# State-space layer and ternary feed-forward on eight cores: first product of block pairs as seven half-size products, one ring of x buffers, second rounding on ScalarE

## The chip, the cores and the metric

The kernel runs as one program on the 8 cores (NeuronCores) of one Trainium2 chip. The metric is the device time of one execution in microseconds (us), taken on the slowest core. A core has TensorE (matmuls into PSUM), VectorE (DVE in the profile), ScalarE (ACT), GpSimd (POOL) and SyncE (SP), each with its own in-order instruction stream; they meet through semaphores. A wait in a stream holds up all that is queued behind it.

## What is computed

x is 4 sequences of 8192 tokens by D = 1024, f32. The reference, cut to what matters:

```python
x = x + attn(layernorm(x))       # u = x W_in^T (N = 64); h_t = Abar h + Bbar u_t; y = (C h) W_out^T
x = x + ffn(layernorm(x))

def quant_weight(w):             # ternary: -s, 0, +s
    s = clip(mean(abs(w)), EPS, None)
    return clip(round(w / s), -1, 1) * s
def quant_act(x):                # integers -127..127 with a scale for each token
    scale = 127 / clip(max(abs(x), axis=-1), EPS, None)
    return round(x * scale) / scale
def ffn(x):                      # 1024 -> 4096 -> 1024
    h = gelu(quant_act(x) @ quant_weight(w1).T)
    return quant_act(h) @ quant_weight(w2).T
```

## The kernel before

Each sequence is split over two cores. The even core owns its first 33 blocks of 128 tokens (FIRST), the odd core the other 31 (LATER). The odd core first computes the state that the scan starts from with 33 short steps over the first part's x. After that all cores do the same: load and make ternary both weight matrices (as FP8, in units of 2^-9), and then pass over their blocks.

One block c takes these steps, and each engine's program is an order written out by hand:

- `stats(c)` (VectorE, 528): mean and variance; `inv1` (GpSimd): the power -0.5; `xnorm(c)` (ScalarE, 393): normalized x in BF16; `txn(c)` (SP, 205): its DMA transposition.
- `mmu(c)` (TensorE, 763): u; `scan(c)` (VectorE, 546); `hbf(c)` (ScalarE, 400): the state in BF16; `mmy(c)` (TensorE, 773, 774): y.
- `mix(c)` (VectorE, 550 to 579): x2 = x + y into a buffer of its own, its statistics, row maximum, scale, and rounding by adding and subtracting 1536 in F16, to `k1`; `inv2_` on GpSimd stands within it; `tk1(c)` (SP, 211): DMA transposition.
- `mm1(c)` (TensorE, 751): eight groups of 512 output columns, eight matmuls each (128x128 stationary, 512 columns), over three PSUM banks; `gelu(c, gi)` (ScalarE, 380) takes each group out into `h`.
- `hmax(c, j)` (VectorE, 583): row maximum of 1024 columns of h; `hquant(c)` (VectorE, 588 to 601): a chain of five small operations for the scale, then `k2h` (599: multiply, add 1536, 4096 columns) and `k2b` (601: subtract); `tk2(c)` (SP, 219): DMA transposition.
- `mm2(c)` (TensorE, 786): 32 x 2 matmuls of 512 columns into `pout` (two banks); `fin(c)` (VectorE, 607): x2 + a2 * pout, stored by GpSimd (318).

From block 2 on TensorE runs `mm1(b)`, `mmu(b+2)`, `mmy(b+1)`, `mm2(b-1)`. Blocks 0 and 1 and the weights are interleaved ahead of that. VectorE runs `fin(b-2)`, `stats(b+3)`, four `hmax(b)`, `mix(b+1)`, `scan(b+2)`, `hquant(b)`. x is loaded by GpSimd (297) into a ring of three buffers and x2 goes into a ring of four. `mm2(c)` waits until `fin(c-1)` has read `pout`.

All buffers in SBUF are views into one array, `BIG`, so that is the name that most rows show; PSUM tensors are `pm` (first product), `pout`, `py`, `pu`.

Of the kernel before, what the change touches and what calls it, by code (L numbers as in the profile page):

```python
# [26 lines left out]
VE_TILES = (0, 4)  # L27


def build_nc():  # L30
# [42 lines left out]
    xbs = [at(28, D), at(96, D), at(100, D)]  # L73
    x2 = [at(176, D), at(180, D), at(48, D), at(104, D)]
# [6 lines left out]
    k1he, k1hs = at(168, D, F16), at(56, D, F16)  # L81
    k1be = [at(170, D, BF16), at(188, D, BF16)]
    k1bs = [at(58, D, BF16), at(60, D, BF16)]
    k1T = [at(184 + 2 * i, D, BF16).rearrange("p (k t) -> p k t", k=8) for i in range(2)]
    k2h = [at(188, H, F16), at(64, H, F16)]
    k2b = [at(188, H, BF16), at(64, H, BF16)]
    k2T = [at(o, H, BF16).rearrange("p (m t) -> p m t", m=32) for o in (32, 72)]

    def xb_of(c):
        return xbe[c] if c < 2 else xbs[(c - 2) % 3]  # L90
# [34 lines left out]
    amx, cl, rr, q1, am2, cl2, r2, sc2 = [s1(34 + i) for i in range(8)]  # L125
    am4 = s1(42, 4)
# [13 lines left out]
    pm1 = [nc.alloc_psum_tensor(f"pm1{i}", [128, 512], F32).ap() for i in range(3)]  # L140
    pout = nc.alloc_psum_tensor("pout", [128, 1024], F32).ap()
# [10 lines left out]
            + ["xe0", "xe1"] + [f"xl{i}" for i in range(3)] + [f"od{i}" for i in range(4)]  # L152
            + [f"{n}{i}" for n in ("xT", "kT", "hT") for i in range(2)]
            + ["id", "pxn", "exn", "pk1", "ek1"])

    with ExitStack() as ctx:
# [15 lines left out]
        def wait_xb(eng, c):  # L172
            if c < 2:
                eng.wait_ge(S[f"xe{c}"], 16)
            else:
                eng.wait_ge(S[f"xl{(c - 2) % 3}"], 16 * ((c - 2) // 3 + 1))


        def sync_program(sp, later):
# [40 lines left out]

            tk2(0)
# [6 lines left out]
            for b in range(2, own):  # L228
                if b + 3 < own:
                    txn(b + 3)  # L230
                if 4 <= b + 1 < own:
                    tk1(b + 1)
                tk2(b)

# [9 lines left out]
        def gpsimd_program(g, later):  # L244
# [6 lines left out]
            g.memset(tu, TU)  # L251
            g.iota(ident_f, pattern=[[-1, 128]], base=0, channel_multiplier=1,
# [58 lines left out]
            load(5)  # L311
            inv1(3)
            inv1(4)
            inv2_(3)
            for b in range(2, own + 2):
                c = b - 2
                g.wait_ge(S["out"], c + 1)
                g.dma_start(out=out_d[c], in_=x2[c % 4]).then_inc(S[f"od{c % 4}"], 16)  # L318
                if b + 3 < own:
                    inv1(b + 3)  # L320
                if 4 <= b + 1 < own:
                    inv2_(b + 1)
# [14 lines left out]
        def scalar_program(s, later):  # L337
# [120 lines left out]
            for b in range(2, own):  # L458
                for gi in range(4):
                    gelu(b, gi)  # L460
                if b + 3 < own:
                    xnorm(b + 3)
                for gi in range(4, 8):
                    gelu(b, gi)
                if b + 2 < own:
                    hbf(b + 2)
# [10 lines left out]
        def vector_program(v, later):  # L477
# [72 lines left out]
            def mix(c):  # L550
                v.wait_ge(S["y"], c + 1)
                xx = x2[c % 4]
                xc, k1h = (xce, k1he) if c < 2 else (xcs, k1hs)
                if c >= 4:
                    v.wait_ge(S[f"od{c % 4}"], 16 * (c // 4))
# [19 lines left out]
                v.tensor_scalar(k1h, xc, q1, MAGIC, op0=ALU.mult, op1=ALU.add); D_()  # L575
                if c >= 4:
                    v.wait_ge(S[f"kT{c % 2}"], 16 * (c // 2 - 1))
                v.tensor_scalar(k1b_of(c), k1h, -MAGIC, None, op0=ALU.add)
                D_().then_inc(S["k1"], 1)

            def hmax(c, j):
                v.wait_ge(S["gelu"], 8 * c + 2 * j + 2)
                v.tensor_reduce(am4[:, j:j + 1], h_of(c)[:, j * 1024:(j + 1) * 1024], AX.X,  # L583
                                ALU.max, apply_absolute_value=True)

            def hquant(c):
                D_()
                v.tensor_reduce(am2, am4, AX.X, ALU.max); D_()
# [297 lines left out]
```

## Time and profile before

| | |
|---|---|
| median of 3 runs | 1107.63 us (1107.47 to 1111.19) |
| profiled execution | 1110.62 us; span of its slowest core (6) 1109.1 us |
| even cores (33 blocks), spans | 1104.3, 1105.5, 1105.7, 1109.1 us |
| odd cores (31 blocks), spans | 1097.5, 1098.3, 1096.1, 1096.8 us |
| busy, core 6 | TensorE 88%, VectorE 63%, ScalarE 29%, GpSimd 10% |

The span runs from the first instruction of a core to its last. Busy shares are of the whole span. "Granted clock" is the share of full clock that TensorE was given in a stretch; 1.00 is 2.4 GHz and 0.50 is 1.2 GHz. In a row, L751 is line 751, `out<-in` names what is written and read, and the bracket says how long the engine was idle before and what ended that. A timeline merges instructions of one kind that follow each other; "x64" is their number. "SPq" is the queue of SyncE, whose time is the issue of a DMA, not its transfer.

### The profile page before, as it was taken

Reading aid. Unit: us, or ns where it says so; the run is one execution under the profiler, and the core shown is the slowest. Engines: PE = TensorE matmul, PEld = TensorE weight load, DVE = VectorE, ACT = ScalarE, POOL = GpSimd, SP = SyncE. Lnnn points to the kernel's source line nnn. Section 1 sums busy time; section 2 is a strip of 40 time slices with the busy share of each in tenths; the row PEclk is TensorE's granted clock in tenths of the full one; section 3 lists DMA queues with packets and bytes.
Section 4 is the critical chain, followed back from the end, with each engine's and each line's share of the span. In section 5 each row is a group of like instructions: output and inputs, shape, how many; then the busy total and the mean of one; then the engine's idle time right before and its main releaser. Section 6 shows DMA issues by size and latency. Waiting matters only on the chain.

```text
span 1109.1 us, 13658 instructions; the slowest of 8 cores (1096.1 to 1109.1 us)
## 1 busy us (share of the span) xinstructions
PE 970.7 (88%) x4590; PEld 436.2 (39%) x4590; DVE 695.9 (63%) x1050; ACT 323.3 (29%) x378; POOL 114.6 (10%) x187
## 2 busy tenths in 40 slices
PE   0116719899999999999999999999999999999995
PEld 0102204344444444444444444444444444444442
DVE  0257887686666666666666666666666666666630
ACT  2279972322222222222222222222222222222110
POOL 1004021111111111110011111111111100000000
PEclk9998859999999999999999999999999999999998
DMA  5946824344444434334444444444443333333340
GB/s 177 337 153 228 378 57 114 77 100 91 95 95 95 92 90 94 83 90 95 96 95 95 95 95 96 95 94 88 96 86 86 85 90 84 90 71 67 67 95 38
DMA packets 213950, 120.53 MB, mean 109 GB/s; under 512 B 203184, under 2 KB 203184, under 8 KB 211824
## 3 DMA queue, kind: packets, MB, share of 16 engines
q1 hardware_dynamic: 202352, 52.45, 25.8%
q0 software_dynamic: 11520, 67.11, 17.6%
q8 instruction: 40, 0.66, 0.2%
q14 instruction: 38, 0.31, 0.1%
HBM read 51.38 MB, written 17.30 MB: 62 GB/s over the span
## 4 chain that ended last, share of the span: by engine, by line
PE 82%; DVE 5%; ACT 4%; DMA 4%; issue 2%; ACTq 1%; DVEq 1%; SPq 1%; POOL 0%; POOLq 0%
PE pm L751 39%; PE pout L786 39%; DMA BIG<-woutT 3%; ACT BIG L361 2%; PE pu L763 2%; ACT BIG L366 1%; PE py L773 1%; DVE BIG L633 1%; ACTq L367 1%; PE py L774 1%; ACTq L363 1%; DMA BIG<-xh 1%; ACT BIG L380 0%; DVE BIG L628 0%; DVE BIG L629 0%
## 5 line engine op out<-in xcount | busy, mean ns | idle before, releaser
L751 PE MATMUL pm<-BIG 128*128 128x512 fp8e4 x2112 | 470.4, 384 | 19.6 <-DVE BIG L629 9.3
L786 PE MATMUL pout<-BIG 128*128 128x512 fp8e4 x2112 | 464.1, 380 | 22.8 <-DMA BIG<-BIG 20.0
L751 PEld LDWEIGHTS pm<-BIG 128*128 128x128 bf16 x2112 | 207.8, 99 | 276.6 <-issue 34.4
L786 PEld LDWEIGHTS pout<-BIG 128*128 128x128 bf16 x2112 | 204.4, 98 | 279.6 <-issue 39.6
L583 DVE TENSOR_REDUCE sm<-BIG 128x1 f32<-128x1024 f32 x132 | 160.5, 1219 | 230.2 <-ACT BIG L380 230.2
L380 ACT ACTIVATE BIG<-pm,sm 128x512 f32<-128x512 f32 x264 | 179.9, 686 | 377.5 <-PE pm L751 376.1
L400 ACT CAST hb_s<-h_s 64x128 bf16<-64x128 f32 x33 | 9.8, 298 | 287.3 <-DVEq L548 287.3
L599 DVE TENSOR_SCALAR BIG<-BIG,sm 128x4096 f16<-128x4096 f32 x33 | 77.6, 2353 | 5.4 <-issue 1.0
L288 POOL TENSOR_TENSOR sm<-sm 128x1 f32<-128x1 f32 x33 | 28.3, 859 | 443.1 <-DVE sm L563 443.1
L607 DVE SCALAR_TENSOR_TENSOR BIG<-pout,sm,BIG 128x1024 f32<-128x1024 f32 x33 | 42.3, 1283 | 28.9 <-PE pout L786 22.9
L794 PE MATMUL pout<-BIG 128*128 128x128 bf16 x32 | 4.0, 305 | 61.5 <-ACT BIG L393 47.7
L318 POOL DMA_DIRECT2D out<-BIG x33 | 18.1, 549 | 361.7 <-DVE BIG L607 361.7
L393 ACT ACTIVATE BIG<-BIG,sm 128x1024 bf16<-128x1024 f32 x33 | 40.6, 1231 | 49.0 <-POOL sm L281 49.0
L361 ACT ACTIVATE BIG<-BIG 128x4096 fp8e4<-128x4096 f32 (+1 forms) x14 | 47.2, 3372 | 7.1 <-DMA BIG<-w1t 5.4
L366 ACT ACTIVATE BIG<-BIG,sm 128x4096 f32<-128x4096 f32 x12 | 45.6, 3798 | 6.4 <-DVEq L622 5.8
L601 DVE TENSOR_SCALAR BIG<-BIG 128x4096 bf16<-128x4096 f16 x33 | 40.5, 1227 | 4.3 <-issue 0.5
L565 DVE TENSOR_REDUCE sm<-BIG 128x1 f32<-128x1024 f32 x33 | 40.3, 1220 | 2.4
L556 DVE TENSOR_TENSOR BIG<-BIG,py 128x1024 f32<-128x1024 f32 x33 | 39.9, 1211 | 0.7 <-PE py L774 0.5
L633 DVE TENSOR_SCALAR BIG<-BIG 128x4096 fp8e4<-128x4096 f32 x12 | 27.5, 2294 | 6.7 <-ACTq L367 5.6
L279 POOL TENSOR_TENSOR sm<-sm 128x1 f32<-128x1 f32 x33 | 22.5, 682 | 81.4 <-DVE sm L538 81.4
L794 PEld LDWEIGHTS pout<-BIG 128*128 128x128 bf16 x32 | 3.1, 137 | 62.8 <-issue 62.8
L575 DVE TENSOR_SCALAR BIG<-BIG,sm 128x1024 f16<-128x1024 f32 x33 | 24.9, 753 | 2.5
(83 smaller groups left out, 389.4 us busy)
## 6 DMA issues: line engine op xcount, KB each, us to landing
out<-BIG POOLq DMA_DIRECT2D x33, 512.0 KB, 6.5
BIG<-w1t POOLq DMA_DIRECT2D x8, 2048.0 KB, 35.3
BIG<-w2t POOLq DMA_DIRECT2D x8, 2048.0 KB, 17.9
BIG<-xh POOLq DMA_DIRECT2D x31, 512.0 KB, 4.0
BIG<-BIG SPq DMA_TRANSPOSE x95, 3.1
BIG<-xh SPq DMA_DIRECT2D x2, 512.0 KB, 16.1
BIG<-winT SPq DMA_DIRECT2D x1, 256.0 KB, 25.6
BIG<-woutT SPq DMA_DIRECT2D x1, 256.0 KB, 30.4
```

The costliest lines, as they stand in the source:

```text
L361: s.activation(junk[:, 0:part], wtile[w][:, 0:part], AF.Abs, bias=0.0, scale=1.0, accum_out=acc[:, w:w + 1], saturate=False)
L366: s.activation(wtile[w], wtile[w], AF.Relu, bias=tu, scale=cw)
L380: s.activation(h_of(c)[:, gi * 512:(gi + 1) * 512], pm1[G % 3], AF.Gelu, bias=0.0, scale=a1[c % 4]).then_inc(S["gelu"], 1)
L393: s.activation(xn_of(c), xb_of(c), AF.Identity, bias=nb1[c % 2], scale=inv[c % 2]).then_inc(S["xn"], 1)
L556: v.tensor_tensor(xx, xb_of(c), py, ALU.add)
L565: v.tensor_reduce(amx, xc, AX.X, ALU.max, apply_absolute_value=True); D_()
L583: v.tensor_reduce(am4[:, j:j + 1], h_of(c)[:, j * 1024:(j + 1) * 1024], AX.X, ALU.max, apply_absolute_value=True)
L599: v.tensor_scalar(k2h[c % 2], h_of(c), sc2, MAGIC, op0=ALU.mult, op1=ALU.add)
L601: v.tensor_scalar(k2b[c % 2], k2h[c % 2], -MAGIC, None, op0=ALU.add)
L607: v.scalar_tensor_tensor(x2[c % 4], pout, a2[c % 4], x2[c % 4], op0=ALU.mult, op1=ALU.add).then_inc(S["out"], 1)
L751: m = t.matmul(pm1[G % 3], k1T[c % 2][:, k, :], t1T[gi][:, k, :], start=(k == 0), stop=(k == 7))
L786: i = t.matmul(pout[:, d * 512:(d + 1) * 512], k2T[c % 2][:, m, :], t2T[m // 4][:, m % 4, d * 512:(d + 1) * 512], start=(m == 0), stop=(m ...
```

## The change

It has three parts, all from block 5 (`PAIR0`) on, with new orders for blocks 2 to 4.

**Seven products.** Blocks are taken in pairs (c0, c1), 14 on an even core, 13 on an odd one. In the first product the pair's 256 tokens, the 1024 inputs and each 1024 output columns (group j of four) are cut in halves: a 2x2 by 2x2 block product, which is done with seven half-size products M1 to M7 in place of eight (Winograd's form of Strassen's method). Each is four matmuls of 512 columns (`prod`). The sums of x (`xsums`: four additions of 512 columns in F16 a pair, on VectorE) go into `sa`; the sums of weights (`wsums`, `wsum3`: four subtractions of 2048 FP8 columns for each j, once, on VectorE in blocks 2 to 4) into `tb`. Partial results are kept in h: ScalarE copies the bank `pp` out after M1, M6 and M7 (`sn1`, `sn2`, `sn3`), TensorE goes on accumulating in it, VectorE adds another bank to the copies (`add11`, `add22`, `add12`), and Gelu then works in place in SBUF (`g11`, `g22`, `g12`) or from the bank (`g21`).

**One ring of x.** `xs` has seven buffers, from the load through x2 and the result to the store; from block 7 on SP issues the loads. `mm2` uses two pairs of banks in turn.

**Second rounding on ScalarE.** The multiply-and-add of 4096 columns (599) becomes `k2round`, an ACTIVATE with bias 1536. k1 is transposed in F16, without a BF16 copy.

Cut to its core, with the orders that matter:

```diff
+PAIR0 = 5
+NX = 7
-    xbs = [at(28, D), at(96, D), at(100, D)]
-    x2 = [at(176, D), at(180, D), at(48, D), at(104, D)]
+    xs = [at(o, D) for o in (176, 180, 28, 48, 60, 96, 100)]
...
+    pout, pout2 = pw[:, 0:1024], pw[:, 1024:2048]
+    pm1 = [pw[:, 1024:1536], pw[:, 1536:2048], pr]
+    pp = [pw[:, 0:512], pw[:, 1024:1536]]
+    pq = [pw[:, 512:1024], pw[:, 1536:2048]]
...
# SyncE, in place of txn(b + 3), tk1(b + 1), tk2(b)
+            for q in range(pairs(own)):
+                txn(c1 + 2); load(c0 + 4); txn(c0 + 4); tk1(c0 + 2)
+                tk2(c0); tk1(c1 + 2); load(c1 + 4); tk2(c1)
...
# ScalarE
+            def k2round(c):
+                s.wait_ge(S["hs"], c - 1)
+                s.wait_ge(S[f"hT{c % 2}"], 16 * (c // 2))
+                s.activation(k2h[c % 2], h_of(c), AF.Identity, bias=magic,
+                             scale=sc2[c % 2]).then_inc(S["k2h"], 1)
+            def keep(g, src, dst, made, sem):
+                s.wait_ge(S[made], g + 1)
+                s.copy(dst, src).then_inc(S[sem], 1)
+                sn1(0) g11(0) sn2(0) sn1(1) sn3(0) g22(0) g11(1)
+                xnorm(c1 + 2)
+                sn2(1) g12(0) g21(0)
+                hbf(c0 + 2)
+                for j in (2, 3):
+                    sn3(j-1) sn1(j) g22(j-1) g11(j) sn2(j) g12(j-1) g21(j-1)
+                sn3(3) g22(3) g12(3) g21(3)
+                hbf(c1 + 2) xnorm(c0 + 4) k2round(c0) k2round(c1)
...
# VectorE
+            def wsums(j):
+                v.tensor_tensor(tb_f[j][0], b12, b11, ALU.subtract, saturate=False); D_()
+                v.tensor_tensor(tb_f[j][1], b22, tb_f[j][0], ALU.subtract, saturate=False); D_()
+                v.tensor_tensor(tb_f[j][2], b21, tb_f[j][1], ALU.subtract,
+                                saturate=False).then_inc(S["tsum"], 1)
+            def addto(g, c, j, d, src, made, kept, sem):
+                o = h_of(c)[:, j * 1024 + d * 512:j * 1024 + (d + 1) * 512]
+                v.wait_ge(S[made], g + 1)
+                v.wait_ge(S[kept], g + 1)
+                v.tensor_tensor(o, src, o, ALU.add).then_inc(S[sem], 1)
+            for b in range(2, PAIR0):
+                fin(b - 2)                          # from b = 3
+                stats(b + 3) hmax(b, 0) hmax(b, 1) scan(b + 2)
+                hmax(b, 2) hmax(b, 3) hscale(b) mix(b + 2) k2int(b)
+                b == 2: wsums(0) wsums(1)      b == 3: wsums(2) wsums(3)
+                b == 4: wsum3(0) wsum3(1) among the hmax, then wsum3(2) wsum3(3) xsums(0)
+            for q in range(pairs(own)):
+                fin(3 if q == 0 else c1 - 4)
+                add11(0) stats(c1 + 2) add22(0) scan(c0 + 2) add11(1) add12(0) add22(1)
+                add11(2) hmax(c0, 0) hmax(c1, 0) add12(1) add22(2)
+                add11(3) hmax(c0, 1) stats(c0 + 4) add12(2) hmax(c1, 1) add22(3)
+                scan(c1 + 2) hmax(c0, 2) add12(3) hmax(c1, 2) hmax(c0, 3)
+                hscale(c0) hmax(c1, 3) hscale(c1) mix(c0 + 2) k2int(c0)
+                fin(c0 - 2)                         # from q = 1
+                mix(c1 + 2) k2int(c1) xsums(q + 1)
...
# TensorE
+            for b in range(2, PAIR0):
+                mm1(b, 0, 4); mmu(b + 2); mm1(b, 4, 8); mmy(b + 2)
+                if b >= 3:
+                    mm2(b - 1)
+            def prod(bank, a, w, start, sem):
+                for k in range(4):
+                    m = t.matmul(bank, a[:, k, :], w[:, k, :], start=start and k == 0,
+                                 stop=k == 3, skip_group_check=not start)
+                m.then_inc(S[sem], 1)
+                m1(0) m5(0) m2(0) m6(0) m1(1) m7(0) mmu(c0 + 2) m5(1) m2(1) m6(1) m3(0) m4(0) m7(1)
+                for j in (2, 3):
+                    m1(j) m5(j) m2(j) m6(j) m3(j-1) m4(j-1) m7(j)
+                    if j == 2: mmy(c0 + 2)
+                mmu(c1 + 2) m3(3) m4(3)
+                mm2(c0 - 2, 0, 16) mmy(c1 + 2) mm2(c0 - 2, 16, 32) mm2(c1 - 2)
+                # q == 0: mm2(4) alone, with mmy(c1 + 2) in its middle
+            mm2(own - 2)
+            mm2(own - 1)
```

In the last pair the steps of blocks that do not exist are left out. What the seven products wait for: M1(0) of pair 0 for `fin(3)`, M1(1) for `fin(c1-4)`, M1(j) from j = 2 for g21(j-2); M5(0) for the first x sum, M5(j) from j = 2 for add12(j-2); M2(j) for add11(j-1); M6(j) for sn1(j); M7(j) for sn2(j); M3(j) for add22(j); M4(j) for sn3(j). `mm2(own-1)` no longer waits for `fin(own-2)`.

## Rows read from the trace of the kernel before

**Rows 1.** Busy time in a stretch (columns named in the first row), core 6.
```profile
core 6: us, PE busy (x) PEld busy (x) DVE busy (x) ACT busy (x) POOL busy (x), PEclk, DMA share, GB/s
308.00:1057.00 749.00, 749.00 (x3581) 338.15 (x3580) 490.44 (x769) 175.31 (x257) 69.17 (x123) 1.00 0.41 89
```
**Rows 2.** Timeline of one block on TensorE: start us, us, engine, line.
```profile
506.63 13.98 PE L751 MATMUL pm<-BIG 128*128 128x512 fp8e4 x64
...
520.53 0.63 PE L763 MATMUL pu<-BIG,winTb 128*64 128x128 bf16 x8
...
521.63 13.99 PE L786 MATMUL pout<-BIG 128*128 128x512 fp8e4 x64
...
535.46 13.98 PE L751 MATMUL pm<-BIG 128*128 128x512 fp8e4 x64
```
**Rows 3.** Groups by line: busy us, mean ns, idle before and releaser.
```profile
L380 ACT ACTIVATE BIG<-pm,sm 128x512 f32<-128x512 f32 x264 | 179.9, 686 | 377.5 <-PE pm L751 376.1 <-issue 1.4
L366 ACT ACTIVATE BIG<-BIG,sm 128x4096 f32<-128x4096 f32 x12 | 45.6, 3798 | 6.4 <-DVEq L622 5.8
L393 ACT ACTIVATE BIG<-BIG,sm 128x1024 bf16<-128x1024 f32 x33 | 40.6, 1231 | 49.0 <-POOL sm L281 49.0
L601 DVE TENSOR_SCALAR BIG<-BIG 128x4096 bf16<-128x4096 f16 x33 | 40.5, 1227 | 4.3 <-issue 0.5
L556 DVE TENSOR_TENSOR BIG<-BIG,py 128x1024 f32<-128x1024 f32 x33 | 39.9, 1211 | 0.7 <-PE py L774 0.5 <-issue 0.2
L546 DVE TENSOR_TENSOR_SCAN h_s<-abt,h_s,pu 64x128 f32<-64x128 f32 x32 | 15.1, 472 | 15.7 <-PE pu L763 8.5 <-issue 7.1
L404 ACT CAST BIG<-pout 128x1024 bf16<-128x1024 f32 x2 | 2.0, 1012 | 4.8 <-PE pout L794 4.8
```
**Rows 4.** Timeline of VectorE: stats and two hmax, then a mix and a scale.
```profile
209.07 0.69 DVE L531 BATCH_NORM_STATS2 sm<-BIG 128x6 f32<-128x512 f32 x1 [0.19 <-issue]
...
210.88 2.35 DVE L583 TENSOR_REDUCE sm<-BIG 128x1 f32<-128x1024 f32 x2
...
1041.60 1.21 DVE L556 TENSOR_TENSOR BIG<-BIG,py 128x1024 f32<-128x1024 f32 x1
...
1049.33 0.16 DVE L588 TENSOR_REDUCE sm<-sm 128x1 f32<-128x4 f32 x1 [0.17 <-issue]
...
1050.44 2.35 DVE L599 TENSOR_SCALAR BIG<-BIG,sm 128x4096 f16<-128x4096 f32 x1
```
**Rows 5.** Timeline where one engine hands over to another.
```profile
508.67 0.69 ACT L380 ACTIVATE BIG<-pm,sm 128x512 f32<-128x512 f32 x1 [6.13 <-PE pm L751]
...
510.34 0.69 ACT L380 ACTIVATE BIG<-pm,sm 128x512 f32<-128x512 f32 x1 [0.98 <-PE pm L751]
...
511.13 1.22 DVE L583 TENSOR_REDUCE sm<-BIG 128x1 f32<-128x1024 f32 x1 [0.81 <-ACT BIG L380]
...
1081.76 1.28 DVE L607 SCALAR_TENSOR_TENSOR BIG<-pout,sm,BIG 128x1024 f32<-128x1024 f32 x1 [6.91 <-PE pout L786]
...
1083.19 13.97 PE L786 MATMUL pout<-BIG 128*128 128x512 fp8e4 x64 [1.54 <-DVE BIG L607]
```
**Rows 6.** Timeline of blocks 2 and 5, and transposes by issue to landing (page).
```profile
200.33 12.26 PE L751 MATMUL pm<-BIG 128*128 128x512 fp8e4 x56
...
210.41 1.26 SPq L205 DMA_TRANSPOSE BIG<-BIG  x1
...
275.97 13.98 PE L751 MATMUL pm<-BIG 128*128 128x512 fp8e4 x64
...
BIG<-BIG SPq DMA_TRANSPOSE x95, 3.1
```
**Rows 7.** TensorE after waits, and stretches: cores 6 and 1.
```profile
163.22 12.73 PE L786 MATMUL pout<-BIG 128*128 128x512 fp8e4 x48 [19.97 <-DMA BIG<-BIG]
...
243.15 13.40 PE L751 MATMUL pm<-BIG 128*128 128x512 fp8e4 x56
...
240.00:245.00 5.00, 3.40 (x15) 1.35 (x16) 3.46 (x7) 0.30 (x2) 0.81 (x2) 0.71 0.02 3
...
195.00:200.00 5.00, 1.88 (x15) 0.89 (x13) 1.20 (x3) 0.30 (x1) 0.00 (x0) 1.00 0.27 52
```

More of the change, by code:

```diff
@@ L708, in vector_program @@
-                if 4 <= b + 1 < own:
-                    mix(b + 1)
-                if b + 2 < own:
-                    scan(b + 2)
-                if b < own:
-                    hquant(b)
+                stats(b + 3)
+                hmax(b, 0)
+                hmax(b, 1)
+                scan(b + 2)
+                if b == 4:
+                    wsum3(0)
+                hmax(b, 2)
+                if b == 4:
+                    wsum3(1)
+                hmax(b, 3)
+                hscale(b)
@@ new lines, in vector_program, with add11, add22, add12 @@
+                mix(b + 2)
+                k2int(b)
+                if b == 2:
+                    wsums(0)
+                    wsums(1)
+                elif b == 3:
+                    wsums(2)
+                    wsums(3)
+                else:
+                    wsum3(2)
+                    wsum3(3)
+                    xsums(0)
+            for q in range(pairs(own)):
+                c0, c1 = PAIR0 + 2 * q, PAIR0 + 2 * q + 1
+                def add11(j):
+                    addto(4 * q + j, c0, j, 0, pr, "M2", "sn1", "a11")
+                def add22(j):
+                    addto(4 * q + j, c1, j, 1, pq[j % 2], "M5", "sn3", "a22")
+                def add12(j):
+                    addto(4 * q + j, c0, j, 1, pq[j % 2], "M3", "sn2", "a12")
+                fin(3 if q == 0 else c1 - 4)
+                add11(0)
+                if c1 + 2 < own:
+                    stats(c1 + 2)
+                add22(0)
+                if c0 + 2 < own:
+                    scan(c0 + 2)
+                add11(1)
+                add12(0)
+                add22(1)
+                add11(2)
+                hmax(c0, 0)
+                hmax(c1, 0)
+                add12(1)
+                add22(2)
+                add11(3)
+                hmax(c0, 1)
+                if c0 + 4 < own:
+                    stats(c0 + 4)
+                add12(2)
+                hmax(c1, 1)
+                add22(3)
+                if c1 + 2 < own:
+                    scan(c1 + 2)
+                hmax(c0, 2)
+                add12(3)
+                hmax(c1, 2)
+                hmax(c0, 3)
+                hscale(c0)
+                hmax(c1, 3)
+                hscale(c1)
+                if c0 + 2 < own:
+                    mix(c0 + 2)
+                k2int(c0)
+                if q > 0:
+                    fin(c0 - 2)
+                if c1 + 2 < own:
+                    mix(c1 + 2)
+                k2int(c1)
+                if c1 + 2 < own:
+                    xsums(q + 1)
@@ L715, in _ @@
+            for c in range(own - 3, own):
+                fin(c)
         @block.vector
```

368 lines of the change are left out of this document (286 added, 82 removed).

## The prediction

> **What bounds the kernel now.** I read the stretches first: between 308 and 1057 us TensorE is busy in every microsecond at granted clock 1.00, VectorE 65% and ScalarE 23% [rows 1]. The timeline of one block then shows what TensorE does: first product from 506.63, u and y from 520.53, second product from 521.63, next block at 535.46, so 28.83 us a block; 64 matmuls of 512 columns go from 521.63 to 535.46, 0.216 us each [rows 2]. TensorE's work is the time there; the other engines and the DMAs are under it. So a matmul left out is worth 0.216 us, if nothing makes TensorE wait instead. The profiled core has 33 blocks, its odd-numbered neighbours 31 and a longer start; they end earlier and lose one pair less, so they don't set the time.
>
> **Sizes used for the new work.** One product of the seven is four matmuls: 0.86 us. A copy PSUM to SBUF of 512 columns ("keep"): the 1024-column one took 1.01 [rows 3]; bounds 0.51 (half) and 0.69 (the Gelu of as many columns); I take 0.59, since 1024 to 4096 columns cost 0.84 ns a column on ScalarE (lines 393, 366) and the rest is fixed. Gelu out of SBUF: 0.69 as out of PSUM [rows 3]; below 0.62 (half of line 393), above 0.80 (0.43 plus line 393's fixed 0.37). An addition of 512 columns: 0.68, from half of line 556's 1.21 (0.61) and VectorE's other 512-column operation, 0.69 [rows 3, 4]; I take the nearer to the latter. The rounding on ScalarE, 128x4096: 3.80, as line 366. On VectorE an operation that waits for nothing starts about 0.08 early: two hmax in 2.35, one 1.22, and stats holds the engine 209.07 to 210.88, 1.81. mix holds it 7.7 (1041.60 to 1049.33), the scale of a block 1.1 (to 1050.44) [rows 4], scan 0.65 (0.47 [rows 3] and its drain). Handovers: the eighth matmul's slot ends at 506.63 + 8 x 0.216 = 508.36 and Gelu starts 508.67, so 0.31; ScalarE to VectorE 0.10 (510.34 + 0.69 to 511.13), and I take the same back; VectorE to TensorE 0.15 (1081.76 + 1.28 to 1083.19) [rows 5].
>
> **The pair, saving.** Four column groups of seven products of four matmuls, 112, replace 128: 16 x 0.216 = 3.45 us a pair, 14 pairs, 48.3 us.
>
> **The pair, what it adds.** Before, TensorE fed three banks and only Gelu stood behind it. Now all engines work through written orders in which 12 keeps, 12 additions and 16 Gelus alternate, and TensorE waits for them. Each of the four column groups j holds one chain that starts at the end of M2(j), so their waits add up:
> - j=0: handover 0.31, add11 0.68, 0.10, g11 0.69, sn2 (queued behind g11) 0.51, 0.15 = 2.44, before M7(0). TensorE has M6 and M1(1), 1.73, in between: waits 0.7.
> - j=1: the same, with xnorm (1.15) ahead of sn2: 3.59, against M6, M3, M4 = 2.59: waits 1.0. Then g12(0) and g21(0) (1.22) before M1(2), against M7: 0.36.
> - j=2: 0.31, add11 0.68, two hmax and add12(1) 2.88, 0.10, g12 0.69, g21 0.61, 0.15 = 5.42, before M1(3). TensorE: four products and y, 3.92: waits 1.5.
> - j=3: 0.31, add11 0.68, then hmax, stats and add12(2) on VectorE 3.55, 0.10, g12 0.69, g21 0.61, sn3(3) 0.51, 0.10, add22(3) 0.68, 0.15 = 7.38, before M3(3). TensorE: four products and u, 4.02: waits 3.4. This is the largest: a 1.81 us stats that nobody waits for stands ahead of an addition that everybody waits for.
> - After the products y of the second next block needs x2 of the first, whose mix stands behind the rest of that queue: after add22(3) a scan, four hmax, add12(3), two scales and the x2 addition, 9.4. TensorE has M3, M4 and half an mm2, 8.8: waits 0.65.
>
> Together 7.55 against 3.45 saved: +4.1 us a pair. Hidden: both roundings on ScalarE, under the two second products (27.7 us); the four sums of transposed x (0.42 to 0.68 each), ready about 1 us before M5(0) wants them if the transposition lands in 3.1 us [rows 6] (if that cover goes, each us late is 13 us in all); the loads, which move from POOL's queue to SP's, where each stands behind transposes but has most of a pair before its stats; the second block's k1 transpose, which stands behind the k2 transpose of the first on SP, due 9 us before it. POOL keeps stores and powers, none of which TensorE waits for sooner than before. The x ring and second output bank remove waits that are nearly nil; the last one (1.5, ahead of 1083.19 [rows 5]) goes.
>
> **The change-over, blocks 2 to 4.** TensorE now wants u(4) after half of block 2's product. The transposition that it needs is issued at 210.41 [rows 6] and queued behind the same work as before, so it lands at 213.6 where TensorE stands at 200.33 + 6.9: about 6 us. The block's last Gelu then ends at 222.1, its scale at 224.6. From there VectorE is the bound. Up to fin(3), for which M1 of the first pair waits, its queue holds 3 mix 23.0, 3 conversions (line 601) 3.9, 16 subtractions of FP8 weights, 3 fin 3.7, 2 stats 3.6, 8 hmax 9.4, 2 scales 2.2, 2 scans 1.3, the x sums 1.8. A subtraction has 2048 columns and two sources: line 556 takes 1.21 for 1024, so 2.28 (2.3 with its drain); no row shows two-source FP8, and the bound below is half, since one-source operations do better than line 556 per column (line 601). Nearest is the two-source row: 36.8. In all 85.7, and 2.3 of waits (xnorm and Gelu behind stats): 312.8 for M1, where the first product of block 5 starts at 275.97 now [rows 6]: +36.9.
> The Trainium skill, VectorE: DVE Perf Modes, "What auto-detection actually checks", lets a two-source operation double its rate only if every tensor is 16-bit. By it the sum stands as made here; by the lower bound of the rows it would be 18.4 us smaller. No run yet shows which.
>
> **First and last pair.** Pair 0 has one second product instead of two under VectorE's two mixes: counted from the last product, mix starts at +6.1, and 7.7 + 1.3 + 7.7 + 3.1 + 0.7 (mix, conversion, mix, transposition, x sum with handover) end at +26.6; TensorE would be at M5(0) at 13.8 + 0.5 + 0.65 + 0.86, +15.8: waits 10.7. Pair 13 has no u, y, stats or xnorm: by the same chains 5.5 of waits.
>
> **Sum.** 36.9 + (4.1 + 10.7) + 12 x 4.1 + (5.5 - 3.45) - 1.5 = +101.4. The clock: after 20 us without work 48 matmuls took 12.73 instead of 10.35 [rows 7], 2.4 lost; two new long waits (about 8 and 11 us) have no other wait behind them: +4.8. Total +106.2. The profiled execution took 1110.62 (span 1109.1), so 1217; its distance to the median of 1107.63 is 3, so **1214**.
>
> **Rivals.**
> - *TensorE loses its clock in every pair.* Around M3(3) it has one u (0.57 us) in 3.9. For: on core 1 a like stretch ended at 243.15 with the clock at 0.71, and 56 matmuls took 13.40 for 12.26: with y 1.5 lost. Against: core 6 had the same waits at 195 to 200 and stayed at 1.00 (2.4 GHz; 0.50 is 1.2) [rows 7]. Price 1.5 to 2.4 x 12: 1232 to 1243. The Trainium skill, TensorE: Matmul & The Clock Gate, "HAM oscillation — how this bites in real kernels", has a loop pay in every iteration for waits that are long enough; no row here shows that in a steady loop. Chance 0.18.
> - *Cheap subtractions* (two columns a cycle, 1.14): 16 x 1.15 = 18.4 less, 1196. Only the missing row speaks for it. 0.11.
> - *Waits in the pairs half as long* (handovers shorter, operations overlapping more): 14 x 3.8 less, 1161. 0.10.
> - *TensorE stays the bound in the pairs*, the one that ends faster: each chain j is over before TensorE needs it, and 48.3 comes back in full. For: up to add12(3) VectorE has fin 1.2, 12 additions 7.7, 2 stats 3.6, 2 scans 1.3 and 5 hmax 5.9, 19.7 us, in 25.8 of products, so the load fits. Against: order, not load, makes the waits. With the change-over as above -2, 1105; with it at the lower bound 1087. It decides where the waits fall under 1.5 a pair. 0.09 (0.02 of it within 0.5%).
> - *Forecast* 0.52.
>
> **Numbers.** Unknown sizes move a pair by -1.1 (3 keeps, 5 Gelus, 7 additions in the chains at their lower bounds) to +0.9: 1199 to 1227; with the subtractions and the restarts at their least 1176; with the clock rival 1255. Down to 1160 the half-wait case is in. Range 1160 to 1255; outside remain the faster case and some 0.1 of worse. A measurement tells 0.5% (5.5 us) from no change. Faster 0.07, same 0.02, slower 0.91.
>
> **What would show it.** The step from one pair's first product to the next near 61.7 us; TensorE idle about 7.5 us in it, 3.4 of that ahead of the second-to-last product, released by add22; FP8 subtractions near 2.3 us; first pair's M1 near 313, M5(0) of the second pair 10 us late, released by VectorE. Wrong it is if a pair takes 57.7 or less, or if the subtractions take 1.2; a clock under 1.00 in the middle means the first rival.

## The result, and the profile after

The changed kernel takes 1220.98 us (median of 4 runs, 1218.05 to 1226.02), the kernel before on the same chip 1107.55 us (4 runs, 1106.08 to 1111.19): the ratio is 1.1024, 95% interval 1.0978 to 1.1069. It is slower by 113 us; forecast were 1214, between 1160 and 1255. The profiled execution, the slowest of the four, took 1226.02 us, span 1224.5 on core 4 (33 blocks); the even cores 1217.3 to 1224.5, the odd ones 1201.5 to 1203.6. Executions in which the cores of one die ran at a lower clock than the others stand in no ratio below; experiment 2's profile is of such a one, and is read on a core of the other die.

Busy shares of the whole span, from the page. TensorE was at 88% on the core profiled before; VectorE and ScalarE were at 63% and 29%.

```profile
PE 957.0 (78%) x4366; PEld 414.2 (34%) x4366; DVE 785.1 (64%) x1259; ACT 520.6 (43%) x577; POOL 101.6 (8%) x162
```

The same stretch view as [rows 1], over the pairs:

```profile
core 4: us, PE busy (x) PEld busy (x) DVE busy (x) ACT busy (x) POOL busy (x), PEclk, DMA share, GB/s
395.00:1040.00 645.00, 577.27 (x2663) 250.30 (x2662) 435.81 (x756) 278.05 (x354) 46.15 (x82) 0.97 0.38 83
```

TensorE, which was busy in every microsecond [rows 1], now stands idle for 68 of 645 us, and no other engine is busy all the time (VectorE 68%, ScalarE 43%). The granted clock is 0.97 and no longer 1.00.

One pair on TensorE, the view of [rows 2]: start us, us, engine and line (L1090 the seven products, L1010 and L1020 u and y, L1040 the second product), and in brackets the wait ahead and what ended it.

```profile
511.84 1.02 PE L1090 MATMUL pw<-BIG 128*128 128x512 fp8e4 x4 [0.75 <-ACT BIG L530]
...
518.69 1.02 PE L1090 MATMUL pw<-BIG 128*128 128x512 fp8e4 x4 [0.84 <-ACT BIG L530]
519.88 1.89 PE L1090 MATMUL pw<-BIG 128*128 128x512 fp8e4 x8 [0.17 <-ACT BIG L560]
...
527.89 1.89 PE L1090 MATMUL pw<-BIG 128*128 128x512 fp8e4 x8 [1.26 <-ACT BIG L560]
...
534.02 0.63 PE L1010 MATMUL pu<-BIG,winTb 128*64 128x128 bf16 x8
537.92 1.89 PE L1090 MATMUL pw<-BIG 128*128 128x512 fp8e4 x8 [3.26 <-DVE BIG L877]
...
547.21 0.37 PE L1020 MATMUL py<-woct,hb_s 64*128 64x512 bf16 x1 [0.50 <-DVEq L686]
```

These are the six waits of the forecast, in its order: 0.7, 1.0, 0.36, 1.5, 3.4 and 0.65 were forecast; 0.57 to 0.75, 0.84, 0.17, 1.26, 3.26 and 0.50 are there. L877 ahead of M3(3) is the addition add22(3). A pair whose clock holds takes 61.69 us (547.74 to 609.43, from the last 96 matmuls of its second products to those of the next pair), against 57.66 for two blocks before.

The change-over and the first two pairs, same view:

```profile
215.25 1.03 PE L1010 MATMUL pu<-BIG,winTb 128*64 128x128 bf16 x8 [7.70 <-DMA BIG<-BIG]
...
257.05 3.57 PE L998 MATMUL pw<-BIG 128*128 128x512 fp8e4 x8 [17.01 <-ACT BIG L430]
...
317.58 3.57 PE L1090 MATMUL pw<-BIG 128*128 128x512 fp8e4 x8 [6.45 <-DVE BIG L751]
...
350.41 1.89 PE L1090 MATMUL pw<-BIG 128*128 128x512 fp8e4 x8 [3.11 <-DVE BIG L877]
354.36 8.75 PE L1040 MATMUL pw<-BIG 128*128 128x512 fp8e4 x32 [2.06 <-ACT BIG L560]
...
379.19 1.86 PE L1090 MATMUL pw<-BIG 128*128 128x512 fp8e4 x4 [7.66 <-DVEq L867]
```

Block 5's first product, at 275.97 before [rows 6], starts at 317.58. VectorE waits for only 4.0 of the 90 us from 227.6 to there (for Gelu in block 3, 1.28 and 2.71), and its new work is in these groups of the stretch from 200 to 320 us (busy us, mean ns):

```profile
L850 DVE TENSOR_TENSOR BIG<-BIG 128x2048 fp8e4<-128x2048 fp8e4 x4 | 9.2, 2292 | 0.3
L857 DVE TENSOR_TENSOR BIG<-BIG 128x2048 fp8e4<-128x2048 fp8e4 x4 | 9.2, 2292 | 0.7 <-issue 0.5
```

With lines 848 and 849 they make 16 subtractions of 2.29 us. The other new operations, on the page of the profile: a keep 0.58, Gelu out of SBUF 0.72, an addition 0.69, the rounding on ScalarE 3.79.

```profile
L530 ACT COPY BIG<-pw 128x512 f32<-128x512 f32 x168 | 95.4, 576 | 282.6 <-PE pw L1090 282.6
L534 ACT ACTIVATE BIG<-BIG,sm 128x512 f32<-128x512 f32 x168 | 121.3, 722 | 197.1 <-DVE BIG L877 197.1
L877 DVE TENSOR_TENSOR BIG<-pw,BIG 128x512 f32<-128x512 f32 x112 | 77.2, 689 | 114.9 <-ACT BIG L530 97.9
L511 ACT ACTIVATE BIG<-BIG,sm 128x4096 f16<-128x4096 f32 x31 | 116.3, 3794 | 20.6 <-DVE sm L733 20.6
```

### The profile page after: what moved, and what is told of

The parts are those of the page before. It is cut to its first block, busy times and chain, and to the rows that moved or that the text cites. A ratio compares the mean times of both kernels' runs of the same rounds, so it can differ in the third digit from the quotient of the medians.

```text
span 1224.5 us, 14782 instructions; the slowest of 8 cores (1201.5 to 1224.5 us)
## 1 busy us (share of the span) xinstructions
PE 957.0 (78%) x4366; PEld 414.2 (34%) x4366; DVE 785.1 (64%) x1259; ACT 520.6 (43%) x577; POOL 101.6 (8%) x162
## 3 DMA queue, kind: packets, MB, share of 16 engines
q1 hardware_dynamic: 206096, 66.08, 27.1%
## 4 chain that ended last, share of the span: by engine, by line
PE 48%; DVE 19%; issue 10%; ACT 8%; DVEq 7%; DMA 6%; ACTq 1%; SPq 1%; POOL 0%; POOLq 0%
PE pw L1040 30%; PE pw L1090 12%; DVE BIG L877 4%; PE pr L1090 4%; DVE sm L717 3%; DMA BIG<-woutT 2%; ACT BIG L560 2%; DVEq L661 2%; DMA BIG<-w2t 2%; ACT BIG L443 1%; ACT BIG L530 1%; DVE BIG L685 1%; ACT BIG L411 1%; ACT BIG L534 1%; DVE BIG L777 1%
## 5 line engine op out<-in xcount | busy, mean ns | idle before, releaser
L1040 PE MATMUL pw<-BIG 128*128 128x512 fp8e4 x2112 | 470.3, 384 | 24.3 <-DMA BIG<-BIG 20.6
L1090 PE MATMUL pw<-BIG 128*128 128x512 fp8e4 x1344 | 328.5, 390 | 96.8 <-DVE BIG L877 42.4
L1040 PEld LDWEIGHTS pw<-BIG 128*128 128x128 bf16 x2112 | 207.7, 99 | 286.4 <-issue 48.7
L1090 PEld LDWEIGHTS pw<-BIG 128*128 128x128 f16 x1344 | 127.6, 99 | 273.6 <-issue 144.4
L530 ACT COPY BIG<-pw 128x512 f32<-128x512 f32 x168 | 95.4, 576 | 282.6 <-PE pw L1090 282.6
L534 ACT ACTIVATE BIG<-BIG,sm 128x512 f32<-128x512 f32 x168 | 121.3, 722 | 197.1 <-DVE BIG L877 197.1
L717 DVE TENSOR_REDUCE sm<-BIG 128x1 f32<-128x1024 f32 x132 | 157.1, 1212 | 19.5 <-ACT BIG L430 15.9
L877 DVE TENSOR_TENSOR BIG<-pw,BIG 128x512 f32<-128x512 f32 x112 | 77.2, 689 | 114.9 <-ACT BIG L530 97.9
L511 ACT ACTIVATE BIG<-BIG,sm 128x4096 f16<-128x4096 f32 x31 | 116.3, 3794 | 20.6 <-DVE sm L733 20.6
L998 PE MATMUL pw<-BIG 128*128 128x512 fp8e4 x216 | 57.0, 418 | 40.5 <-ACT BIG L430 26.6
L877 DVE TENSOR_TENSOR BIG<-pr,BIG 128x512 f32<-128x512 f32 x56 | 38.7, 691 | 75.9 <-PE pr L1090 75.9
L751 DVE SCALAR_TENSOR_TENSOR BIG<-pw,sm,BIG 128x1024 f32<-128x1024 f32 x33 | 42.2, 1280 | 53.4 <-PE pw L1040 52.9
L1090 PE MATMUL pr<-BIG 128*128 128x512 fp8e4 x224 | 58.4, 383 | 0.0
## 6 DMA issues: line engine op xcount, KB each, us to landing
BIG<-woutT SPq DMA_DIRECT2D x1, 256.0 KB, 29.8
```

The costliest lines, as they stand in the source:

```text
L511: s.activation(k2h[c % 2], h_of(c), AF.Identity, bias=magic, scale=sc2[c % 2]).then_inc(S["k2h"], 1)
L530: s.copy(dst, src).then_inc(S[sem], 1)
L534: s.activation(part(c, j, d), part(c, j, d), AF.Gelu, bias=0.0, scale=a1[c % 4]).then_inc(S[sem], 1)
L717: v.tensor_reduce(am4[c % 2][:, j:j + 1], h_of(c)[:, j * 1024:(j + 1) * 1024], AX.X, ALU.max, apply_absolute_value=True)
L751: v.scalar_tensor_tensor(x_of(c), po, a2[c % 4], x_of(c), op0=ALU.mult, op1=ALU.add).then_inc(S["out"], 1)
L877: v.tensor_tensor(o, src, o, ALU.add).then_inc(S[sem], 1)
```

## The experiments

They came in three sets, in which the kernel before took 1113.5, 1112.1 and 1111.4 us, so ratios to it are compared; one per cent is 11.1 us. Each diff is against the changed kernel unless it says otherwise.

**1. Without the pairs.** All blocks go one by one, in the new order of blocks 2 to 4. The ring and the rounding on ScalarE stay; the sums of weights and of x are gone, and the second product has one pair of banks again.

```diff
         def pairs(own):
-            return (own - PAIR0) // 2
+            return 0
-            for b in range(2, PAIR0):
+            for b in range(2, own):
```

> All blocks from 2 on as blocks 2 to 4 of the changed kernel, no pair: eight products, no FP8 subtractions, no kept partial sums; the ring of x and the rounding on ScalarE stay, mix runs two blocks ahead. My theory (the seven products with their sums and order cost all but some 10 us): 28.8 us a block again, and only the wait for u(4) (7.7 us, now in block 2) and some 2 us of Gelu behind the rounding stay, 1113 to 1120 us. Rival (the ring, the longer SP queue or the 3.8 us rounding on ScalarE is a good part of the loss): blocks of 29.5 us and more, 1130 us and up.

Measured: ratio 1.0115 (1.0040 to 1.0191), some 13 us slower than before where 5 to 12 were expected, so of the 113 us about 100 belong to the seven products. A steady block takes 28.93 us, two 57.86, against 28.83 and 57.66 before. The second product in three blocks on end shows it:

```profile
245.00 13.97 PE L1023 MATMUL pw<-BIG 128*128 128x512 fp8e4 x64
273.93 13.99 PE L1023 MATMUL pw<-BIG 128*128 128x512 fp8e4 x64
302.86 13.99 PE L1023 MATMUL pw<-BIG 128*128 128x512 fp8e4 x64
```

Block 5's first product stands behind the one at 273.93, so at 287.8: the new order of blocks 2 to 4 costs 11.8 us by itself (waits of 4.38, 2.00 and 1.65 us, and matmuls at a fallen clock behind the first two), and the subtractions with what they hold up the other 29.8 of block 5's delay. In a steady block the ring and the moved rounding cost 0.1 us at most, 3 us in all; the rival of 29.5 us a block falls.

**2. TensorE kept at work in the longest wait.** Five more copies of u's matmuls, into the same bank and overwritten by the true ones, run ahead of M3(3).

```diff
                 if c1 + 2 < own:
-                    mmu(c1 + 2)
+                    mmu(c1 + 2, 5)
```

> The changed kernel, with u of the pair's second next block computed six times in place of once ahead of M3(3), so TensorE works through the 3.3 us wait; nothing that anyone waits for comes later. Theory (TensorE loses its clock after that wait in 8 of 13 pairs and pays 1.6 us each time): M3(3) and M4(3) take 1.9 us in every pair, 12 us less, 1209. Rival (the slow products there are something else, or cost nothing because VectorE is the bound behind them): unchanged, 1221 within 4.

Measured: ratio 1.0939 (1.0866 to 1.1012), 9 us under the changed kernel's, where 12 were expected. On core 4 the granted clock is 1.00 from 440 to 1000 us, M3(3) and M4(3) take 1.89 in every pair, and a pair takes 61.69:

```profile
591.49 2.42 PE L1011 MATMUL pu<-BIG,winTb 128*64 128x128 bf16 x40
595.39 1.89 PE L1094 MATMUL pw<-BIG 128*128 128x512 fp8e4 x8 [1.03 <-DVE BIG L877]
```

The work fills 2.3 of the 3.3 us and moves nothing later, so what it gained is the clock alone. The intervals of the two ratios overlap; the rows carry the reading more than the 9 us do.

**3. The order named by the forecast.** `stats(c0 + 4)` moves from ahead of add12(2) to behind add12(3).

```diff
                 hmax(c0, 1)
-                if c0 + 4 < own:
-                    stats(c0 + 4)
                 add12(2)
...
                 add12(3)
+                if c0 + 4 < own:
+                    stats(c0 + 4)
```

> The changed kernel with one operation group moved on VectorE: stats(c0+4) from ahead of add12(2) to behind add12(3). Same work. Theory (order makes the waits): the wait ahead of M3(3) falls from 3.3 to 1.5 us, the wait ahead of y in the middle of the second product grows from 0.5 to 2.3 us, so a pair stays the same but for the falls of the clock, which a shorter wait should make rarer: 1209 to 1221. Rival (VectorE's load makes them): the wait ahead of M3(3) stays at 3.3 us.

Measured: ratio 1.1030 (1.0938 to 1.1122), no change, at the upper end of what was expected. Its timeline on TensorE, one pair on core 2:

```profile
656.89 1.89 PE L1090 MATMUL pw<-BIG 128*128 128x512 fp8e4 x8 [1.38 <-DVE BIG L877]
658.61 7.07 PE L1040 MATMUL pw<-BIG 128*128 128x512 fp8e4 x32
668.44 0.37 PE L1020 MATMUL py<-woct,hb_s 64*128 64x512 bf16 x1 [2.76 <-DVEq L686]
668.96 22.58 PE L1040 MATMUL pw<-BIG 128*128 128x512 fp8e4 x96
```

The wait ahead of M3(3) fell from 3.27 to 1.38 by the 1.9 us that stats is long, and came back one wait later: y, at 0.50 before, now waits 2.41 to 2.76, since mix stands behind stats. In 3 of the 11 pairs with this wait the clock fell there: the next 96 matmuls took 22.58 for 20.89, and 23.60 and 23.44 in the two pairs after. So an operation moved within a full queue moves the wait with it.

**4. A new order on all engines.** On TensorE M5, M3 and M4 go to where their inputs are ready, M7 behind u; two chunks of the second product fill the wait ahead of M4(3) and M3(3), and y stands behind the whole of it. VectorE makes add22(0) a place later, splits the maxima and makes both mix ahead of the conversions; ScalarE takes g21 ahead of g12, and xnorm later. On SP the loads and transposes are re-ordered.

```diff
                 m1(0)
-                m5(0)
                 m2(0)
+                m5(0)
...
-                m7(0)
                 if c0 + 2 < own:
                     mmu(c0 + 2)
+                m7(0)
...
-                    m5(j)
                     m2(j)
+                    m4(j - 1)
                     m6(j)
                     m3(j - 1)
-                    m4(j - 1)
+                    m5(j)
...
+                if q > 0:
+                    mm2(c0 - 2, 0, 2)
+                m4(3)
                 m3(3)
-                m4(3)
...
-                    mm2(c0 - 2, 0, 16)
+                    mm2(c0 - 2, 2, 32)
                     if c1 + 2 < own:
                         mmy(c1 + 2)
-                    mm2(c0 - 2, 16, 32)
```

> The changed kernel with the same work in other orders on all engines: at least two other products between any two products of one bank, add12 ahead of hmax and stats, g21 ahead of g12, xnorm(c1+2) behind g12(1), four matmuls of the second product ahead of M4(3) and M3(3), y behind the second product, both mix ahead of the conversions. Theory (four chains of order): no wait of TensorE in a pair but some tenths, 54.2 to 54.8 us a pair in place of 61.7 and the clock at full rate; change-over and the wait of the second pair stay: 1109 to 1118 us. Rival (VectorE is the real bound of a pair, 48 us of work and its handovers): TensorE waits for the sums of x at each pair's start instead, 57 us a pair and more, 1140 and up.

Measured: ratio 1.0394 (1.0321 to 1.0467), 70 us under the changed kernel, 33 or more above what was expected. A pair takes 56.62 us (430.12 to 486.74, core 2); one wait of 1.87 to 2.21 us is left in each, ahead of M3(0), which needs add22(0). All engines' timeline there, in order of time:

```profile
722.88 0.34 SPq L245 DMA_DIRECT2D BIG<-xh  x1
...
727.28 0.69 DVE L660 BATCH_NORM_STATS2 sm<-BIG 128x6 f32<-128x512 f32 x1 [3.96 <-DMA BIG<-xh]
...
730.75 4.44 PE L1090 MATMUL pw<-BIG 128*128 128x512 fp8e4 x12 [2.21 <-DVE BIG L877]
```

stats waited for x: SP issued the load at 722.88, 4.4 us ahead, because it stands behind a transposition of k2 that has a wait of its own. VectorE's additions stand behind stats. The rival, VectorE as the bound, had named 57 us a pair and 1140 us or more, which is near what came; the next experiment decides between the two.

**5. The same with that load first.** Against experiment 4:

```diff
-                tk2(c0)
                 load(c1 + 4)
+                tk2(c0)
                 tk2(c1)
```

> The run e4_order with one DMA moved in SP's order: load(c1+4) ahead of tk2(c0), so that it doesn't stand behind the 4.8 us transpose. In e4 VectorE waited 4 us for that load ahead of stats(c1+2), and TensorE 1.9 us for add22(0) behind it, 56.6 us a pair. Theory: the wait goes, 54.5 to 54.8 us a pair, 24 us less than e4: ratio to before near 1.018. Rival (VectorE's chain through both mix is the bound at 56.6): the same 56.6, waiting for the x sums.

Measured: ratio 1.0076 (1.0051 to 1.0101), 105 us under the changed kernel and 35 under experiment 4, where 24 were expected. The rival falls: the same work on VectorE, and the wait is gone. The stretch view of the pairs (experiment 4's core 2 has clock 0.98 in the same stretch):

```profile
core 4: us, PE busy (x) PEld busy (x) DVE busy (x) ACT busy (x) POOL busy (x), PEclk, DMA share, GB/s
440.00:1000.00 560.00, 559.95 (x2673) 250.02 (x2672) 433.66 (x752) 290.45 (x360) 45.28 (x80) 1.00 0.44 97
```

TensorE is busy in every microsecond at clock 1.00 again, now with 112 matmuls in place of 128 in the first product of a pair. VectorE has 77% and ScalarE 52%, and neither makes it wait. The first product of three pairs that follow each other:

```profile
432.82 1.03 PE L1090 MATMUL pw<-BIG 128*128 128x512 fp8e4 x4
...
487.24 1.03 PE L1090 MATMUL pw<-BIG 128*128 128x512 fp8e4 x4
...
541.77 1.03 PE L1090 MATMUL pw<-BIG 128*128 128x512 fp8e4 x4
```

They are 54.42 and 54.53 apart: 3.1 to 3.4 us less than two blocks took (57.66 by [rows 2], 57.86 in experiment 1), so the 16 matmuls come back nearly in full. What is left over the kernel before is the start: M1 of the first pair at 321.13, 45 us later than block 5 there [rows 6] (the even cores of one execution lie up to 7 us apart in this; their means are 46 apart), and waits of 1.99 and 7.93 us in the second pair, 55 in all, against 14 x 3.2 = 45.

**6. The twelve subtractions of the change-over on GpSimd.** Against the changed kernel: GpSimd makes them from the moment that the weights are ready, between its powers and stores, and VectorE keeps the four of `wsum3`.

```diff
+            def wsum(j, i):
+                ...
+                g.tensor_tensor(tb_f[j][i], p, m, ALU.subtract, saturate=False)
...
-                if b == 2:
-                    wsums(0)
-                    wsums(1)
-                elif b == 3:
-                    wsums(2)
-                    wsums(3)
```

> The changed kernel with 12 of the 16 FP8 subtractions done by GpSimd between its powers and stores, from the end of the weights on; the last four (wsum3) stay on VectorE. Theory (VectorE's queue sets the change-over, 2.3 us a subtraction): M1 of the first pair starts 20 to 27 us earlier, near 293 us in place of 317, and the rest is as it was: 1196 to 1202. Rival (the wait for u(4) and the Gelu behind stats set it, or the shared work slows VectorE by as much): less than 8 us.

Measured: ratio 1.0918 (1.0871 to 1.0964), 12 us under the changed kernel where 19 to 25 were expected. M1 of the first pair starts at 310.36, 7 us earlier; each ratio is known to 5 us, so the other 5 need no cause. GpSimd takes 3.82 us for a subtraction, and this happened beside it (all engines' timeline, GpSimd and VectorE):

```profile
237.20 8.05 POOL L339 TENSOR_TENSOR BIG<-BIG 128x2048 fp8e4<-128x2048 fp8e4 x2
...
239.25 2.31 DVE L732 TENSOR_SCALAR BIG<-BIG,sm 128x1024 f16<-128x1024 f32 x1
241.64 3.89 DVE L733 TENSOR_SCALAR BIG<-BIG 128x1024 f16<-128x1024 f16 x1
245.43 3.82 POOL L339 TENSOR_TENSOR BIG<-BIG 128x2048 fp8e4<-128x2048 fp8e4 x1 [0.18 <-issue]
245.72 4.61 DVE L770 TENSOR_SCALAR BIG<-BIG 128x4096 bf16<-128x4096 f16 x1 [0.19 <-issue]
...
270.01 2.31 DVE L732 TENSOR_SCALAR BIG<-BIG,sm 128x1024 f16<-128x1024 f32 x1
...
272.40 3.89 DVE L733 TENSOR_SCALAR BIG<-BIG 128x1024 f16<-128x1024 f16 x1
```

L732 and L733 are the rounding of k1, L770 is the conversion of k2; undisturbed they take 0.75, 0.43 and 1.23. Each ends soon after the subtraction beside it: L733 at 245.53, the pair of subtractions at 245.25; L770 at 250.33, the last subtraction at 249.25. That is 8.4 us lost, and 5.0 more in the two rows of the next block, on the path that the move was to shorten. A maximum of 1024 columns that ran beside a subtraction (226.92, beside the one from 226.68 to 230.50) kept its 1.22. Besides, the powers that xnorm(3) waits for stand behind subtractions in GpSimd's queue, and u(3) waited 6.83 us at 204.18, not 1.41; VectorE ends block 2's scale at 233.0, not 227.6. Twelve subtractions of 2.3 us are 27.6; less 8.4, 5.0 and 5.4 that leaves 8.8, near the 7 us by which M1 is earlier.

**7. Experiments 5 and 6 together,** with u(4) behind the whole first product of block 2, and `wsum3` of j = 2 and 3 within the first pair. The two edits to experiment 5 beside the move to GpSimd:

```diff
                 mm1(b, 0, 4)
-                mmu(b + 2)
+                if b > 2:
+                    mmu(b + 2)
                 mm1(b, 4, 8)
+                if b == 2:
+                    mmu(b + 2)
...
-                    wsum3(2)
-                    wsum3(3)
                     xsums(0)
...
+                if q == 0:
+                    wsum3(2)
                 add22(0)
```

> e6 and e5 together; besides u(4) behind the whole first product of block 2 in place of its middle, and the last two subtractions moved from ahead of the first pair into gaps of VectorE within it. Theory: pairs of 54.6 us, M1 of the first pair near 287, then about 10 us of wait at the second pair, which nothing here removes: 14 x 3.4 gained, some 12 + 10 lost, ratio to before 0.975 to 0.985, 1080 to 1092 where before takes 1108. Rival (gains hide one behind another): above 1.0.

Measured: ratio 0.9943 (0.9916 to 0.9969): faster than the kernel before by about 6 us, and than the changed kernel by 120. Expected was 0.975 to 0.985. M1 of the first pair starts at 304.58, not at the 287 hoped for, and the second pair's wait stays:

```profile
254.36 3.53 PE L1021 MATMUL pw<-BIG 128*128 128x512 fp8e4 x8 [11.63 <-ACT BIG L456]
...
304.58 1.02 PE L1116 MATMUL pw<-BIG 128*128 128x512 fp8e4 x4 [3.29 <-DVE BIG L777]
...
361.60 5.28 PE L1116 MATMUL pw<-BIG 128*128 128x512 fp8e4 x12 [7.97 <-DVEq L894]
```

**8 and 9. The same with all subtractions on VectorE,** once where the changed kernel has them (six after block 2, six after block 3), once spread. Experiment 9 against 8:

```diff
                 if b == 2:
                     wsums(0)
-                    wsums(1)
                 elif b == 3:
+                    wsums(1)
                     wsums(2)
-                    wsums(3)
                 else:
+                    wsums(3)
                     xsums(0)
```

> The version with the new order, the load first, u(4) behind the whole first product of block 2 and the last two subtractions (wsum3 of j = 2, 3) within the first pair, but with all subtractions on VectorE. Theory: in the change-over VectorE is the bound (no gap from 227 to 316 us in the changed kernel), so only what leaves its queue counts: two subtractions of 2.29 us, 4.6 us earlier, M1 of the first pair at about 316 us against 321.1, and the time about 1116 by the base of 1107.5 (ratio to the kernel before 1.002 to 1.006). Of the 15 us by which moving them to GpSimd and these moves together shortened the kernel, then some 10 belong to GpSimd. Rival: TensorE's order is what held it (u(4) waited 5 us for its transposition with two groups of block 2 behind it); then M1 starts at about 309 us and the ratio is 0.997 or less.

> The same, with the twelve subtractions spread: three after block 2 instead of six, six after block 3, three after block 4. Theory: VectorE's sum to the first pair is the same and stays the bound, so TensorE's wait of 15 us for the rounding in block 3 shrinks to about 9 and comes back in blocks 3 and 4; M1 of the first pair within 3 us of the run that is sent with it, ratio 1.000 to 1.006. Rival: what was lost is the lateness of one block's statistics, which holds up Gelu and the rounding behind it on ScalarE; then spreading takes 5 us or more off (ratio under 1.000).

Measured: 1.0001 (0.9972 to 1.0030) and 0.9999 (0.9963 to 1.0035). Against experiment 5, u(4) and the two moved subtractions brought 0.75%, 8 us. M1 starts at 311.11, 10 us earlier: more than the 4.6 of the theory, which counted VectorE's queue alone, and nearer the 12 of its rival, since VectorE also comes to the end of block 2's scale sooner (223.9, not 227.6 as in the changed kernel, and 220.3 to 223.9 on the even cores, not 225.5 to 227.6). Against experiment 7, GpSimd is worth 0.6%, 6 us, where some 10 were expected. Spreading changes nothing, as expected: the wait in block 3 fell from 17.01 to 10.08 us and the one ahead of M1 rose from 4.03 to 8.16.

## Why the prediction was right, step by step

- **The bound and the saving.** Held. The 16 matmuls bring 3.1 to 3.4 us a pair where nothing waits (experiment 5); in the changed kernel the waits take 7.5 against them.
- **The sizes.** All within 0.03 us: subtraction 2.29 for 2.28, keep 0.58 for 0.59, Gelu out of SBUF 0.72 for 0.69, addition 0.69 for 0.68, rounding 3.79 for 3.80. The rival of cheap subtractions falls.
- **The waits in a pair.** Each stands where the chain put it. The idle times sum to 6.6 us, and an interrupted row of 512-column matmuls loses some 0.17 more at each wait (the eight that start at 509.19 would let the next begin at 510.92; it began at 511.84, 0.92 later, with 0.75 shown as idle), which makes the forecast 7.55. The pair takes 61.69; forecast 61.8.
- **"Order, not load, makes the waits"**, said against the rival in which TensorE stays the bound: shown by experiment 5, which has the same operations and takes 54.5 us a pair. That rival's pair, 54.2 us by its sum, came out nearly once the order was changed, and not by the change itself.
- **The clock.** The step that fell short. Its loss in the pairs was kept out of the sum and given 0.18 as a rival; in fact the clock fell in 8 of the 11 pairs in which TensorE waited 3.27 us with 0.6 us of work ahead. The two stretches of the changed kernel around this wait, at the same place of two pairs that follow each other (granted clock in the third column from the end):

```profile
473.00:478.00 5.00, 3.07 (x8) 1.17 (x9) 3.57 (x6) 1.95 (x4) 0.00 (x0) 0.67 0.01 3
...
536.00:541.00 5.00, 3.08 (x15) 1.46 (x16) 3.90 (x6) 2.38 (x5) 0.00 (x0) 1.00 0.01 3
```

  Where it fell, M3(3) and M4(3) took 3.42 and not 1.89 (474.93 and 537.92), and in some pairs the next 32 matmuls 8.15 and not 7.07. Part of it returns, as y then waits for nothing: the pair from 443.80 to 506.45 took 62.65, 1.0 more than one without a fall. From 443.80 to the last pair's first product, at 1129.49, eleven pairs took 685.69, 7.1 more than eleven of 61.69; the pair before adds 2.1, and one of them is 1.9 shorter, as its wait without stats was 1.38: 11 us of lost clock, 1.4 a fall. The rival's price, 1.5 to 2.4, was right near its lower end, but 8 pairs paid it and not 12. By the Trainium skill, TensorE: Matmul & The Clock Gate, "HAM oscillation — how this bites in real kernels", a loop with waits that are long enough pays in every iteration; the trace agrees for 8 pairs of 11, and not for the 3 others, which have the same wait. Experiment 2 takes the falls away, leaves the chain as it is, and gains 9 us.
- **The change-over.** M1 at 312.8 forecast, 317.6 measured. VectorE's queue took what was counted, but began 3.0 us late (block 2's scale ends at 227.6 and not at 224.6). The transposition for u(4), issued at 210.27 as forecast, took 4.7 us to land and not 3.1, so that u(4) started at 215.25 and not at 213.6; and behind that wait u and the next 8 matmuls took 3.9 us for 2.3, a restart at a fallen clock for which the sum had nothing. The other 1.7 us are VectorE's waits for Gelu in block 3, 4.0 where 2.3 were counted: the last 8 matmuls ahead of it took 3.57 for 1.89, again a restart (257.05, behind the wait of 17.01).

```profile
257.58 1.22 DVE L717 TENSOR_REDUCE sm<-BIG 128x1 f32<-128x1024 f32 x1 [1.28 <-ACT BIG L430]
...
261.51 1.22 DVE L717 TENSOR_REDUCE sm<-BIG 128x1 f32<-128x1024 f32 x1 [2.71 <-ACT BIG L430]
```

  A wait of 2.00 (232.30) for Gelu behind the second rounding on ScalarE wasn't in the working either; it stands ahead of the wait of 17.01 and adds nothing to it.
- **First and last pair.** The second pair's wait was 10.7 in the forecast and 7.66 in fact, and not because VectorE was sooner: its chain put M5(0) of the second pair (379.19) 27.1 us after the last product of pair 0, for 26.6 forecast. TensorE came later. The second product of block 4 waits 2.06 for the last Gelu of pair 0 (bank and order), and its first 32 matmuls run at a fallen clock, 8.75 for 7.07; neither was foreseen, and both are nearly paid back by the shorter wait. Last pair: 5.0 us of idle time, with 0.17 at each wait 5.7, for 5.5. Restarts after the two long waits: 1.7 each and not 2.4.
- **The sum.** The profiled run was to have a span of 1109.1 + 106.2 = 1215.3 and had 1224.5, 9.2 more. Longer than forecast: change-over 4.8, falls of the clock 11, block 4's product 3.7, together 19.5. Shorter: the pair without stats 1.9, the second pair's wait 3.0, restarts 1.4, y of pair 0, which waits for nothing, 0.65, 0.07 in each of 12 pairs 0.9, and the time from the last matmul to the end 2.2 (9.8, where core 6 had 11.9 before), together 10.0. The misses of either sign offset each other by half, so the nearness of the median, 7 us over the forecast, is in part luck; the 61.7 us a pair are not.

## What to carry to other kernels

A product left out is worth its time only if every engine in the new chain meets TensorE's order: write each chain from the end of the product that feeds it to the product that needs it, with all that is queued ahead on each engine, and compare it with the work that TensorE has meanwhile. Here that gave each wait to 0.25 us, and it said that the loss was order, so that a new order with the same operations took 105 of 113 us back. Look then at the one-time cost: the 45 us by which the first pair starts later were as much as 14 pairs could save. And moving one operation in a full queue moved its wait to the next reader.

## What the runs showed of the hardware that was not expected

- **A GpSimd operation holds some VectorE operations until it ends.** Beside 3.82 us subtractions on GpSimd (experiment 6), one-source VectorE operations of 1024 to 4096 columns from SBUF to SBUF took 2.31, 3.89 and 4.61 us for 0.75, 0.43 and 1.23, and ended within 1.1 us after it, while a maximum of 1024 columns kept its 1.22. The Trainium skill, SBUF — State Buffer, "SBUF: two separate sides", says that VectorE in a two-port mode and GpSimd hold a shared pair of ports exclusively, for the whole instruction; the trace agrees in that these rows are held to the end of the other instruction and not slowed in proportion. No row shows the mode or the ports.
- **The same wait doesn't always cost the clock.** With 3.27 us of idle time and the same work around it, the granted clock fell in 8 pairs and held in 3 of one execution (0.67 and 1.00 in the rows above), and in experiment 3, on core 2, 2.4 to 2.8 us of idle time ahead of y did so in 3 pairs of 11 (the next 96 matmuls in 22.58, 23.60 and 23.44 us, and in 20.89 in the others). What decides it isn't shown.
- **Left open.** Whether other orders bring the second pair's 8 us back wasn't tried: there only one second product covers two mixes and a transposition. Nor was a later or partial use of the seven products, with the weights' sums made under the loading of the weights.
